# Order of work in a slot of a fused cross-attention and FP4 feed-forward kernel: maximum first on DVE, x1 a slot earlier, weights transposed last on PE

## The chip, the cores and the metric

The kernel runs on one core of a Trainium2 chip. The metric is the device time of one execution in microseconds (us). A core has a matrix engine (TensorE, PE in the profile; its weight loads are PEld), a vector engine (DVE), a scalar engine (ACT), GpSimd (POOL) and SyncE (SP), which issues all DMAs here. Each has its own instruction queue, worked off in order; they wait for one another on semaphores.

## The reference

One transformer layer with float32 inputs: x is 4 x 1024 x 256, the context 4 x 154 x 192, 16 heads of 64, a hidden width of 704.

```
n  = layernorm(x);  q = n Wq;  k, v = ctx Wk, ctx Wv          (16 heads of 64)
x1 = x + softmax(q k^T / 8) v Wo + bo
m  = layernorm(x1);  g = fp4(m) fp4(w_gate)^T;  u = fp4(m) fp4(w_up)^T
h  = silu(g) * u;    out = x1 + fp4(h) fp4(w_down)^T
```

fp4() rounds in blocks of 16 along the last axis: scale = largest magnitude / 6, values to the grid 0, 0.5, 1, 1.5, 2, 3, 4, 6, and back.

## The kernel before, in words

The 4096 rows of x are 32 tiles of 128 rows, worked in pairs; `step(pair, par)` is one tile t = 2 pair + par, written once for every engine and driven by the same `schedule`. A tile has 8 slots (k = 0 to 7), one for each pair of heads, called a unit. All float32 products are made of three: an operand is split into a high part (ACT copies PSUM to an fp32r tile: pT_hi, q_hi, xqT_hi, hqT_hi, xT_hi) and a low part (DVE subtracts that from the PSUM tile: pT_lo and so on, always L637), and PE adds hi x lo, lo x hi and hi x hi.

The tiles are software-pipelined over five tile steps. In slot k of tile t:

- PE makes the **scores** of unit k (L975, ps_s), then **attend** (L998 to L1000): the product of the softmaxed weights of the unit four slots back with B = V Wo, added up over a tile in ps_o. Then **turn_probs** (L985) transposes the weights of the unit two slots back into ps_t, a single PSUM bank, so it waits until DVE has taken the previous unit's pT_lo out of it; then come transposes of the feed-forward operands through ps_m (L865: xn in slot 1, hn in slots 4 and 5; L873: xa of two tiles in slot 6 of even tiles), a quarter of gate and up (L1015, slots 2 to 5), the down product (L1025 to L1027, 18 matmuls, slot 7), a query product of 6 matmuls (L937, slots 0, 1, 2, 4 of even and 0, 1, 3, 6 of odd tiles), and in four tiles of each batch entry the jobs that set up K, V and B of the next one.
- DVE inverts the row sums of the last unit (L746, rsum), makes pT_lo of the unit three slots back, xqT_lo (slot 2) or hqT_lo (slots 5 and 6), and only then takes the **maximum** of this slot's scores (L782, negmax). After it come xT_lo (slot 7 of even tiles), q_lo, x1 and its statistics in slot 4 (L804), the gate quarters (L752, L758, slots 3 to 6), statistics of a later tile in slot 2, and the FP4 scales and rounding (L667 to L692).
- ACT takes pT_hi first, then the other high parts, tanh of the gate quarter, and the exponential of this slot's scores (L610), which needs the maximum; y = copy of x1 (L628) in slot 3.
- POOL multiplies the weights of the last unit by the inverse sums (L472) and does the additions and scaling of the FP4 rounding (L441, L445, L447).

PE's waits inside a slot that the change touches: `attend` of a tile's first unit (slot 4) waits for x1 of the tile before, since it overwrites ps_o; the first gate product waits for xqT_lo; a query product waits for the previous query unit's q_lo; the transposes and the down product in ps_m wait for the last user of that bank (hqT_lo, xT_lo).

```
            def turn_probs(t, u):
                pe.wait_ge(norm_p, PAIRS * t + u + 1)
                if some(PAIRS * t + u):
                    pe.wait_ge(pT_lo, PAIRS * t + u)
```

Of the kernel before, what the change touches and what calls it, by code (L numbers as in the profile page):

```python
# [5 lines left out]
ALU = mybir.AluOpType  # L6
ACT = mybir.ActivationFunctionType
AX_X = mybir.AxisListType.X
# [15 lines left out]
def xattn_ffn_kernel(nc: bass.Bass, x, ctx_768, Wq, Wk, Wv, Wo, bo, w_gate, w_up, w_down, out):  # L24
# [29 lines left out]
    with ExitStack() as stack:  # L54
# [102 lines left out]
        def some(count):  # L157

            return not isinstance(count, int) or count > 0
# [351 lines left out]
        def _(act):  # L511
# [65 lines left out]
            def step(pair, par, own=True, before=True, gate=True, down=True, out_=True, ahead=True, queries=True,  # L577
                     setup=None):
                t = 2 * pair + par
                e, f, d = t - 1, t - 2, t - 3  # L580
                for k in range(SLOTS):
                    if before and k < 3:
                        weights_hi(e, k + PAIRS - 3)
                    if own and k >= 3:
                        weights_hi(t, k - 3)
                    if gate and k == 2:
                        hi_part(xqT[0][:, :, :], parts(ps_m, KT), (xqT_mm, f + 1), xqT_hi)
                    if down and k in (5, 6):
                        r = k - 5
                        hi_part(hqT[0][:, 3 * r:3 * r + 3, :], parts(ps_m, 3), (hqT_mm, 2 * d + r + 1), hqT_hi)  # L590
                    if own and ahead and par == 0 and k == 7:
                        hi_part(xT_all(0), parts(ps_m, 4), (xT_mm, pair + 2), xT_hi)
                    if own and queries and q_unit(par, k - 1) is not None:
                        q_hi_part(pair + par, q_unit(par, k - 1))
                    for job in jobs_before(setup, k):
                        take_hi(job, setup[1])
                    if gate and 3 <= k < Q + 3:
                        q = k - 3
                        quarter = slice(q * QF, (q + 1) * QF)
                        if q == 0 and not some(f):  # L600
                            act.wait_ge(raw_mm, RAW_T[CHUNKS])
                        elif q == 0:
                            act.wait_ge(hq_v, 6 * f - 2)
                        act.wait_ge(gu_mm, Q * f + q + 1)
                        act.activation(eh[:, quarter], ps_g[q % 2][:, 0:QF], ACT.Tanh, scale=0.5).then_inc(th_a, 1)
                    if own:
                        act.wait_ge(max_v, PAIRS * t + k + 1)
                        for s in range(2):
                            h = 2 * k + s
                            ins = act.activation(probs[:, h, 0:M], ps_s[k % 2][:, s * M:(s + 1) * M], ACT.Exp,  # L610
                                                 bias=negmax[:, h:h + 1], accum_out=sums[:, h:h + 1])
                        ins.then_inc(exp_a, 1)
                    if own and ahead and k == 4:
                        layer_norm1_out(t + 3, 1 - par)
                    if before and k == 5:
                        act.wait_ge(ln2_p, 2 * e + 2)
                        if some(e):
                            act.wait_ge(xqT_mm, e)
                        act.activation(xn, x1[1 - par], ACT.Identity, bias=nm2[:, :], scale=rs2[:, :])\
                           .then_inc(xln2_a, 1)  # L620
                    if turn_at(t, k, 0) is not None:
                        chunk_hi(turn_at(t, k, 0))
                    if down and k == 3:
                        at = pair - 2 + par
                        act.wait_ge(x1_v, d + 1)
                        if some(at):
                            act.wait_ge(st_y[1 - par], 16 * at)
                        act.activation(y[1 - par], x1[1 - par], ACT.Copy).then_inc(y_a, 1)  # L628
# [4 lines left out]
        def _(dve):  # L633
# [127 lines left out]
            def step(pair, par, own=True, before=True, gate=True, down=True, out_=True, ahead=True, queries=True,  # L761
                     setup=None):
                t = 2 * pair + par
                e, f, d, c = t - 1, t - 2, t - 3, t - 4
                for k in range(SLOTS):
                    if before and k == 0:
                        invert_sums(e, PAIRS - 1)
                    if own and k >= 1:
# [7 lines left out]
                    if down and k in (5, 6):  # L776
                        r = k - 5
                        lo_part(hqT[1][:, 3 * r:3 * r + 3, :], parts(ps_m, 3), hqT[0][:, 3 * r:3 * r + 3, :],
                                (hqT_hi, 2 * d + r + 1), hqT_lo)
                    if own:  # L780
                        dve.wait_ge(s_mm, PAIRS * t + k + 1)
                        dve.tensor_reduce(negmax[:, 2 * k:2 * k + 2],  # L782
                                          ps_s[k % 2][:, 0:UM].rearrange("p (h m) -> p h m", h=2),
                                          AX_X, ALU.max, negate=True).then_inc(max_v, 1)
                    if out_ and k == 0:
                        dve.wait_ge(d_mm, c + 1)
                        dve.wait_ge(y_a, c + 1)
# [7 lines left out]
                    if turn_at(t, k, 1) is not None:  # L795
                        chunk_lo(turn_at(t, k, 1))
                    if before and k == 4:
                        dve.wait_ge(o_mm, PAIRS * (e + 1))
                        dve.wait_ge(xr_p, e + 1)
                        if some(d + 1):  # L800
                            dve.wait_ge(y_a, d + 1)
                        elif not some(e):
                            dve.wait_ge(raw_mm, RAW_T[3])
                        dve.tensor_tensor(x1[1 - par], xr[1 - par][:, :], ps_o[:, 0:C], ALU.add).then_inc(x1_v, 1)  # L804
                        if some(e):
                            dve.wait_ge(xln2_a, e)
                        stats(x1[1 - par], st2, mv2, ve2, nm2, (x1_v, e + 1), ln2_v, 5 * e)
# [16 lines left out]
                    if before and k == 5:  # L824
                        dve.wait_ge(xln2_a, e + 1)
                        if some(e):
                            dve.wait_ge(xq_p, 4 * e)
                        largest(xn, xri[:, :], xq_v)
                        fp4_scales(xri[:, :], xsc[:, :], xri[:, :], xq_v, 6 * e)
                        dve.wait_ge(xq_v, 6 * e + 3)  # L830
                        dve.tensor_scalar(xri[:, :], xri[:, :], TIES_DOWN, None, ALU.mult).then_inc(xq_v, 1)
                    if gate and k == 6:
                        dve.wait_ge(h_v, Q * (f + 1))
                        largest(eh[:, 0:F], hri[:, :], hq_v)
# [18 lines left out]
        def _(pe):  # L853
# [50 lines left out]
            def make(job, b):  # L904
                kind, i, bank_ = job
                free(bank_)
                ps = BANKS[bank_]
                if kind == "V":
                    if i == 0:
                        pe.wait_ge(ld_w, 32 * b if some(b) else 32)  # L910
                    if isinstance(b, int) and i == 0:
                        pe.wait_ge(pad_p, 4)
                    project(ps, W_sb, 1, i, b, v_mm)
                if kind == "K":
                    if i == 0:
                        pe.wait_ge(ld_w, 32 * b + 16)
                    project(ps, W_sb, 0, i, b, k_mm)
                if kind in ("A", "C", "D"):
                    if isinstance(b, int) and i == 0:
                        pe.wait_ge(ld_wo, 16)  # L920
                    pe.wait_ge(v_ev, KV * b + (2 * i + 2 if kind == "D" else i + 1))
                    for n, block in enumerate(b_blocks(kind, i)):
                        ins = b_block(ps[:, n * C:(n + 1) * C], block)
                    ins.then_inc(b_mm, 1)
                held[bank_] = job_done(kind, i, b)
# [53 lines left out]
# [4 lines that stand above are left out]
                for j in range(blocks(u)):  # L983
                    at = b_at(u, j) * P
                    ins = pe.transpose(ps_t[:, j * P:(j + 1) * P], probs_rows[:, at:at + P], ident[:, :])  # L985
                ins.then_inc(t_mm, 1)
# [43 lines left out]
            def step(pair, par, own=True, before=True, gate=True, down=True, out_=True, ahead=True, queries=True,  # L1030
# [4 lines left out]
                for k in range(SLOTS):  # L1035
# [3 lines left out]
                        attend(e, k + PAIRS - 4, setup if kind == "settle" else None)  # L1039
                    if own and k >= 4:  # L1040
                        attend(t, k - 4, setup if kind in ("start", "roll") else None)
                    if before and k < 2:
                        turn_probs(e, k + PAIRS - 2)
                    if own and k >= 2:
                        turn_probs(t, k - 2)
                    if gate and k == 1:
                        pe.wait_ge(xq_p, 4 * f + 4)
                        m_free((y_v, d), (xqT_lo, f + 1))
# [24 lines left out]
                            pe.wait_ge(q_lo, PAIRS * (pair + par) + max(made))  # L1073
                    for job in jobs_at(setup, k):
                        make(job, setup[1])
                    if turn_at(t, k, 0) is not None:
                        chunk_transposes(turn_at(t, k, 0))

# [28 lines left out]
```

## Time and profile before

| what | value |
|---|---|
| median of 3 runs | 984.53 us (983.6 to 984.84) |
| the profiled execution | 986.75 us, its span 984.9 us |
| PE busy | 857.0 us, 87% of the span |
| DVE busy | 757.5 us, 77% |
| ACT, POOL busy | 534.0 us, 529.5 us |
| chain that ended last | PE 63%, DVE 21%, issue 8%, ACT 4% |
| HBM traffic | mean 23 GB/s |

The span runs from the first to the last instruction of the program, the execution's own time has 1.85 us around it. The start (two tiles) takes some 109 us, then ordinary tiles take 25 to 26 us and those that set up the next batch entry up to 36 us.

### The profile page before, as it was taken

To read this page: it belongs to the slowest core of one execution; us is meant where nothing else is said; L and a number is where in the kernel's file an instruction comes from. 1 tells how busy PE (TensorE), PEld (TensorE's weight loads), DVE (VectorE), ACT (ScalarE), POOL (GpSimd) and SP (SyncE) were. 2 spreads that over 40 slices of the span, in tenths; PEclk is the share of its full clock that TensorE was granted. 3 is DMA by queue.
4 is the path that set the end of the run, shared out by engine and by line. 5 is a ranking of instruction groups with operands and counts; after the bars stand their busy time and mean duration, and the time that the engine had idled before them with its cause. 6 is when DMAs were issued, how large, how long until landed. Compare 5 with 4: busy or idle time off the path is not lost.

```text
span 984.9 us, 21389 instructions
## 1 busy us (share of the span) xinstructions
PE 857.0 (87%) x6254; PEld 812.8 (83%) x6254; DVE 757.5 (77%) x2176; ACT 534.0 (54%) x1879; POOL 529.5 (54%) x677
## 2 busy tenths in 40 slices
PE   4786789999999999989989999989999999999874
PEld 3666789988888998888978888889888888888863
DVE  5857788877778888867878888876877888887762
ACT  4454455556565555556555555556555555655520
POOL 2545666554535656545554656554553656555651
PEclk9888999999999999999999999999999999999986
DMA  7101000001010000001000000001000000000000
GB/s 215 39 11 49 7 17 13 22 13 44 7 33 17 13 23 11 21 14 39 12 28 23 12 22 12 21 8 33 23 7 23 12 18 12 16 11 12 7 11 11
DMA packets 19869, 23.13 MB, mean 23 GB/s; under 512 B 2642, under 2 KB 18234, under 8 KB 19770
## 3 DMA queue, kind: packets, MB, share of 16 engines
q1 hardware_dynamic: 19770, 21.94, 7.2%
q8 instruction: 47, 0.77, 0.3%
q14 instruction: 52, 0.43, 0.1%
HBM read 17.74 MB, written 4.19 MB: 22 GB/s over the span
## 4 chain that ended last, share of the span: by engine, by line
PE 63%; DVE 21%; issue 8%; ACT 4%; POOL 2%; DMA 1%; DVEq 1%; SPq 0%; POOLq 0%; ACTq 0%
PE ps_g L1015 10%; PE ps_q L937 8%; PE ps_s L975 8%; PE ps_t L985 5%; PE ps_o L998 5%; PE ps_o L1000 5%; PE ps_o L999 5%; DVE negmax L782 3%; DVE pT_lo L637 3%; PE ps_m L865 3%; PE ps_g L900 3%; PE ps_m L1025 3%; PE ps_m L1027 2%; PE ps_m L1026 2%; DVE scales L667 2%
## 5 line engine op out<-in xcount | busy, mean ns | idle before, releaser
L472 POOL TENSOR_TENSOR probs<-probs,rsum 128x308 f32<-128x308 f32 x256 | 180.0, 703 | 284.2 <-DVE rsum L746 283.6
L610 ACT ACTIVATE probs<-ps_s,negmax 128x154 f32<-128x154 f32 x512 | 194.7, 386 | 229.4 <-DVE negmax L782 228.2
L998 PE MATMUL ps_o<-B_sb,pT_lo 128*128 128x256 f32 x640 | 183.6, 287 | 38.5 <-DVE x_both L804 33.9
L782 DVE TENSOR_REDUCE negmax<-ps_s 128x2 f32<-128x308 f32 x256 | 121.3, 474 | 78.4 <-PE ps_s L975 76.6
L1000 PE MATMUL ps_o<-B_sb,pT_hi 128*128 128x256 f32 x640 | 181.2, 283 | 0.0
L999 PE MATMUL ps_o<-B_sb,pT_hi 128*128 128x256 f32 x640 | 180.9, 283 | 0.0
L998 PEld LDWEIGHTS ps_o<-B_sb,pT_lo 128*128 128x128 f32 x640 | 121.7, 190 | 45.3 <-issue 42.9
L637 DVE TENSOR_TENSOR pT_lo<-ps_t,pT_hi 128x256 fp32r<-128x256 f32 (+1 forms) x256 | 122.7, 479 | 42.6 <-ACT pT_hi L514 37.4
L985 PE MATMUL ps_t<-ident,probs 128*128 128x128 f32 x640 | 115.0, 278 | 35.9 <-DVE pT_lo L637 35.3
L1015 PE MATMUL ps_g<-WGU,xqT_hi 128*128 128x352 f32 x512 | 136.6, 349 | 3.5 <-DVE B_sb L637 1.9
L514 ACT ACTIVATE pT_hi<-ps_t 128x256 fp32r<-128x256 f32 (+1 forms) x256 | 111.4, 435 | 29.1 <-PE ps_t L985 22.7
L1000 PEld LDWEIGHTS ps_o<-B_sb,pT_hi 128*128 128x128 f32 x640 | 122.1, 191 | 0.0
L999 PEld LDWEIGHTS ps_o<-B_sb,pT_hi 128*128 128x128 f32 x640 | 121.8, 190 | 0.0
L985 PEld LDWEIGHTS ps_t<-ident,probs 128*128 128x128 f32 x640 | 73.8, 141 | 47.3 <-issue 45.7
L610 ACT ACTIVATION_READ_ACCUMULATOR probs<-ps_s,negmax 128x1 f32 x512 | 100.9, 197 | 0.0
L975 PE MATMUL ps_s<-K_hi,q_lo 128*128 128x308 f32 x256 | 87.1, 340 | 3.6 <-issue 3.6
L1015 PEld LDWEIGHTS ps_g<-WGU,xqT_hi 128*128 128x128 f32 x512 | 85.3, 194 | 4.9 <-issue 2.6
L937 PE MATMUL ps_q<-xT_hi,Wq_lo 128*128 128x256 f32 x256 | 80.7, 315 | 8.7 <-DVE q_lo L637 6.1
L1015 PE MATMUL ps_g<-WGU,xqT_lo 128*128 128x352 f32 x256 | 83.5, 326 | 0.0
L441 POOL TENSOR_TENSOR hn<-hn,hc 128x704 f32<-128x704 f32 x32 | 54.4, 1700 | 50.8 <-DVE hc L692 50.8
L975 PE MATMUL ps_s<-K_hi,q_hi 128*128 128x308 f32 x256 | 78.4, 306 | 0.0
L975 PE MATMUL ps_s<-K_lo,q_hi 128*128 128x308 f32 x256 | 78.1, 305 | 0.0
(149 smaller groups left out, 2236.7 us busy)
## 6 DMA issues: line engine op xcount, KB each, us to landing
xa<-in_x_dram SPq DMA_DIRECT2D x33, 128.0 KB, 2.1
xr<-in_x_dram SPq DMA_DIRECT2D x32, 128.0 KB, 2.0
out_dram<-y_xn SPq DMA_DIRECT2D x32, 128.0 KB, 1.7
W_sb<-in_L_xattn_Wk_dram SPq DMA_DIRECT2D x4, 512.0 KB, 4.4
W_sb<-in_L_xattn_Wv_dram SPq DMA_DIRECT2D x3, 512.0 KB, 3.6
probs<-in_L_xattn_Wq_dram SPq DMA_DIRECT2D x1, 1024.0 KB, 7.0
Wo_sb<-in_L_xattn_Wo_dram SPq DMA_DIRECT2D x1, 1024.0 KB, 6.6
VT<-in_ctx_dram SPq DMA_DIRECT2D x1, 384.0 KB
```

The costliest lines, as they stand in the source:

```text
L472: pool.tensor_tensor(unit, unit, rsum[:, 2 * u:2 * u + 2].unsqueeze(2) .to_broadcast([P, 2, M]), ALU.mult).then_inc(norm_p, 1)
L514: act.activation(dst, src, ACT.Copy).then_inc(done, 1)
L610: ins = act.activation(probs[:, h, 0:M], ps_s[k % 2][:, s * M:(s + 1) * M], ACT.Exp, bias=negmax[:, h:h + 1], accum_out=sums[:, h:h + 1])
L637: dve.tensor_tensor(dst, src, hi.bitcast(F32), ALU.subtract).then_inc(done, 1)
L782: dve.tensor_reduce(negmax[:, 2 * k:2 * k + 2], ps_s[k % 2][:, 0:UM].rearrange("p (h m) -> p h m", h=2), AX_X, ALU.max, negate=True).then_ ...
L937: ins = pe.matmul(ps_q[:, 0:2 * P], Wq_sb[w][:, k, u * P:(u + 1) * P], xT[x_][:, k, :], start=(i == 0), stop=(i == len(terms) - 1))
L975: ins = pe.matmul(ps_s[u % 2][:, 0:UM], q_sb[a][:, u, par * P:(par + 1) * P], K_sb[b][:, u, :], start=(i == 0), stop=(i == len(terms) - 1))
L985: ins = pe.transpose(ps_t[:, j * P:(j + 1) * P], probs_rows[:, at:at + P], ident[:, :])
L998: pe.matmul(ps_o[:, 0:C], lo[:, j, :], w[:, 0:C], start=first, stop=False)
L999: pe.matmul(ps_o[:, 0:C], hi[:, j, :], w[:, C:2 * C], start=False, stop=False)
L1000: ins = pe.matmul(ps_o[:, 0:C], hi[:, j, :], w[:, 0:C], start=False, stop=last)
L1015: ins = pe.matmul(ps_g[q % 2][:, 0:2 * QF], x_[:, k, :], WGU[:, k, a, :, q * QF:(q + 1) * QF], start=(i == 0), stop=(i == len(terms) - 1))
```

## The change

It moves three things and adds or removes nothing. On DVE the maximum of a slot's scores comes first in the slot, ahead of the reciprocal and of all low parts. x1 is written as the last DVE work of slot 3 and no longer in slot 4 (its statistics stay there); ACT's copy of x1 into y moves with it from slot 3 to slot 2. On PE `turn_probs` comes behind all products and jobs of the slot. Line numbers move with it: L782 becomes L768, L804 becomes L832, L985 L986 and so on.

```diff
--- before.py
+++ after.py
@@ -620,7 +620,7 @@
                            .then_inc(xln2_a, 1)
                     if turn_at(t, k, 0) is not None:
                         chunk_hi(turn_at(t, k, 0))
-                    if down and k == 3:
+                    if down and k == 2:
                         at = pair - 2 + par
                         act.wait_ge(x1_v, d + 1)
                         if some(at):
@@ -763,6 +763,11 @@
                 t = 2 * pair + par
                 e, f, d, c = t - 1, t - 2, t - 3, t - 4
                 for k in range(SLOTS):
+                    if own:
+                        dve.wait_ge(s_mm, PAIRS * t + k + 1)
+                        dve.tensor_reduce(negmax[:, 2 * k:2 * k + 2],
+                                          ps_s[k % 2][:, 0:UM].rearrange("p (h m) -> p h m", h=2),
+                                          AX_X, ALU.max, negate=True).then_inc(max_v, 1)
                     if before and k == 0:
                         invert_sums(e, PAIRS - 1)
                     if own and k >= 1:
@@ -777,11 +782,6 @@
                         r = k - 5
                         lo_part(hqT[1][:, 3 * r:3 * r + 3, :], parts(ps_m, 3), hqT[0][:, 3 * r:3 * r + 3, :],
                                 (hqT_hi, 2 * d + r + 1), hqT_lo)
-                    if own:
-                        dve.wait_ge(s_mm, PAIRS * t + k + 1)
-                        dve.tensor_reduce(negmax[:, 2 * k:2 * k + 2],
-                                          ps_s[k % 2][:, 0:UM].rearrange("p (h m) -> p h m", h=2),
-                                          AX_X, ALU.max, negate=True).then_inc(max_v, 1)
                     if out_ and k == 0:
                         dve.wait_ge(d_mm, c + 1)
                         dve.wait_ge(y_a, c + 1)
@@ -795,13 +795,6 @@
                     if turn_at(t, k, 1) is not None:
                         chunk_lo(turn_at(t, k, 1))
                     if before and k == 4:
-                        dve.wait_ge(o_mm, PAIRS * (e + 1))
-                        dve.wait_ge(xr_p, e + 1)
-                        if some(d + 1):
-                            dve.wait_ge(y_a, d + 1)
-                        elif not some(e):
-                            dve.wait_ge(raw_mm, RAW_T[3])
-                        dve.tensor_tensor(x1[1 - par], xr[1 - par][:, :], ps_o[:, 0:C], ALU.add).then_inc(x1_v, 1)
                         if some(e):
                             dve.wait_ge(xln2_a, e)
                         stats(x1[1 - par], st2, mv2, ve2, nm2, (x1_v, e + 1), ln2_v, 5 * e)
@@ -829,6 +822,14 @@
                         fp4_scales(xri[:, :], xsc[:, :], xri[:, :], xq_v, 6 * e)
                         dve.wait_ge(xq_v, 6 * e + 3)
                         dve.tensor_scalar(xri[:, :], xri[:, :], TIES_DOWN, None, ALU.mult).then_inc(xq_v, 1)
+                    if before and k == 3:
+                        dve.wait_ge(o_mm, PAIRS * (e + 1))
+                        dve.wait_ge(xr_p, e + 1)
+                        if some(d + 1):
+                            dve.wait_ge(y_a, d + 1)
+                        elif not some(e):
+                            dve.wait_ge(raw_mm, RAW_T[3])
+                        dve.tensor_tensor(x1[1 - par], xr[1 - par][:, :], ps_o[:, 0:C], ALU.add).then_inc(x1_v, 1)
                     if gate and k == 6:
                         dve.wait_ge(h_v, Q * (f + 1))
                         largest(eh[:, 0:F], hri[:, :], hq_v)
@@ -1039,10 +1040,6 @@
                         attend(e, k + PAIRS - 4, setup if kind == "settle" else None)
                     if own and k >= 4:
                         attend(t, k - 4, setup if kind in ("start", "roll") else None)
-                    if before and k < 2:
-                        turn_probs(e, k + PAIRS - 2)
-                    if own and k >= 2:
-                        turn_probs(t, k - 2)
                     if gate and k == 1:
                         pe.wait_ge(xq_p, 4 * f + 4)
                         m_free((y_v, d), (xqT_lo, f + 1))
@@ -1073,6 +1070,10 @@
                             pe.wait_ge(q_lo, PAIRS * (pair + par) + max(made))
                     for job in jobs_at(setup, k):
                         make(job, setup[1])
+                    if before and k < 2:
+                        turn_probs(e, k + PAIRS - 2)
+                    if own and k >= 2:
+                        turn_probs(t, k - 2)
                     if turn_at(t, k, 0) is not None:
                         chunk_transposes(turn_at(t, k, 0))
```

The first place is DVE in slot 2 of an even tile of the steady loop, before and now (with what each row waits for; negmax is the maximum, rsum the reciprocal):

```order
L746 RECIPROCAL rsum<-sums 128x2 [waits exp_a]
L637 TENSOR_TENSOR pT_lo<-ps_t,pT_hi 128x384 [waits pT_hi]
L637 TENSOR_TENSOR xqT_lo<-ps_m,xqT_hi 128x256 [waits xqT_hi]
L781 REGISTER_ALU
L782 TENSOR_REDUCE negmax<-ps_s 128x2 [waits s_mm]
```

```order
L768 TENSOR_REDUCE negmax<-ps_s 128x2 [waits s_mm]
L746 RECIPROCAL rsum<-sums 128x2 [waits exp_a]
L637 TENSOR_TENSOR pT_lo<-ps_t,pT_hi 128x384 [waits pT_hi]
L637 TENSOR_TENSOR xqT_lo<-ps_m,xqT_hi 128x256 [waits xqT_hi]
L636 REGISTER_ALU
L637 TENSOR_TENSOR q_lo<-ps_q,q_hi 128x256 [waits q_hi]
```

The maximum, which waits for the scores of this slot (s_mm), now stands ahead of the two low parts. In slots 5 and 6 it stands in the same way ahead of hqT_lo.

The second place is DVE around the boundary of slots 3 and 4, before and now (x_both is x1):

```order
L758 SCALAR_TENSOR_TENSOR eh<-ps_g,gu 128x176 [waits silu_v]
L746 RECIPROCAL rsum<-sums 128x2 [waits exp_a]
L637 TENSOR_TENSOR pT_lo<-ps_t,pT_hi 128x384 [waits pT_hi]
L781 REGISTER_ALU
L782 TENSOR_REDUCE negmax<-ps_s 128x2 [waits s_mm]
L804 TENSOR_TENSOR x_both<-xr,ps_o 128x256 [waits y_a,xr_p,o_mm]
```

```order
L758 SCALAR_TENSOR_TENSOR eh<-ps_g,gu 128x176 [waits silu_v]
L832 TENSOR_TENSOR x_both<-xr,ps_o 128x256 [waits y_a,xr_p,o_mm]
L767 REGISTER_ALU
L768 TENSOR_REDUCE negmax<-ps_s 128x2 [waits s_mm]
L746 RECIPROCAL rsum<-sums 128x2 [waits exp_a]
L637 TENSOR_TENSOR pT_lo<-ps_t,pT_hi 128x384 [waits pT_hi]
```

x1 has moved ahead of the maximum of slot 4.

The third place is PE in slot 2 of that tile, from the last attend matmuls on, before and now:

```order
L1000 MATMUL ps_o<-B_sb,pT_hi 128x256
L985 MATMUL ps_t<-ident,probs 128x128 [waits pT_lo,norm_p]
L985 MATMUL ps_t<-ident,probs 128x128
L1008 REGISTER_ALU [waits xqT_lo]
L1015 MATMUL ps_g<-WGU,xqT_hi 128x352 [waits h_v]
```

```order
L1001 MATMUL ps_o<-B_sb,pT_hi 128x256
L1009 REGISTER_ALU [waits xqT_lo]
L1016 MATMUL ps_g<-WGU,xqT_hi 128x352 [waits h_v]
...
L938 MATMUL ps_q<-xT_hi,Wq_hi 128x256
L986 MATMUL ps_t<-ident,probs 128x128 [waits pT_lo,norm_p]
L986 MATMUL ps_t<-ident,probs 128x128
L973 REGISTER_ALU [waits q_lo]
```

The transposes of the weights have moved from ahead of the gate product to the slot's end, behind the query product.

## Rows read from the trace of the kernel before

**Rows 1.** Windows view, core 0: one even and the following odd tile (bounds, length, busy us and instructions of each engine, granted clock, DMA share, GB/s).
```profile
559.50:585.50 26.00, 23.84 (x183) 22.83 (x183) 22.45 (x67) 15.03 (x55) 16.03 (x22) 1.00 0.07 22
585.50:610.60 25.10, 23.08 (x181) 22.51 (x180) 20.54 (x62) 14.54 (x54) 14.86 (x20) 1.00 0.04 12
```

**Rows 2.** List of waits, whole span (who waited for whom: us in total, times, longest us).
```profile
PE ps_t L985 <- DVE pT_lo L637: 35.3, 40, 3.2
PE ps_o L998 <- DVE x_both L804: 33.9, 28, 2.4
```

**Rows 3.** Timeline, slot 1 of tile 18 (start us, us, engine, line, operation, out<-in, count).
```profile
561.52 0.30 PE L975 MATMUL ps_s<-K_hi,q_lo 128*128 128x308 f32 x1
...
563.47 0.36 PE L937 MATMUL ps_q<-xT_hi,Wq_lo 128*128 128x256 f32 x1
```

**Rows 4.** Timeline, slot 2 of tile 18, PE and DVE.
```profile
564.06 0.56 DVE L637 TENSOR_TENSOR pT_lo<-ps_t,pT_hi 128x384 fp32r<-128x384 f32 x1 [0.35 <-ACT pT_hi L514]
...
564.26 0.31 PE L975 MATMUL ps_s<-K_hi,q_lo 128*128 128x308 f32 x1
...
564.53 0.41 DVE L637 TENSOR_TENSOR xqT_lo<-ps_m,xqT_hi 128x256 fp32r<-128x256 f32 x1
...
564.89 0.48 DVE L782 TENSOR_REDUCE negmax<-ps_s 128x2 f32<-128x308 f32 x1
...
565.54 0.56 PE L1015 MATMUL ps_g<-WGU,xqT_hi 128*128 128x352 f32 x2
```

**Rows 5.** Timeline, slot 4 of tile 18, and the same product in tile 19; brackets: idle before.
```profile
570.09 0.30 PE L975 MATMUL ps_s<-K_hi,q_lo 128*128 128x308 f32 x1
...
571.66 0.35 PE L998 MATMUL ps_o<-B_sb,pT_lo 128*128 128x256 f32 x1 [0.99 <-DVE x_both L804]
...
598.06 0.36 PE L998 MATMUL ps_o<-B_sb,pT_lo 128*128 128x256 f32 x1 [1.32 <-DVE x_both L804]
```

**Rows 6.** Timeline, end of slot 4 and slot 5 of tile 18, PE and DVE.
```profile
573.73 0.56 DVE L637 TENSOR_TENSOR hqT_lo<-ps_m,hqT_hi 128x384 fp32r<-128x384 f32 x1
...
574.68 0.30 PE L975 MATMUL ps_s<-K_hi,q_lo 128*128 128x308 f32 x1
...
575.30 0.48 DVE L782 TENSOR_REDUCE negmax<-ps_s 128x2 f32<-128x308 f32 x1 [1.01 <-PE ps_s L975]
...
576.17 0.49 PE L985 MATMUL ps_t<-ident,probs 128*128 128x128 f32 x3
...
576.50 0.49 PE L865 MATMUL ps_m<-ident,hn 128*128 128x128 f32 x3
```

**Rows 7.** Timeline, slots 6 and 7 of tile 18, PE and DVE.
```profile
578.85 0.55 DVE L637 TENSOR_TENSOR hqT_lo<-ps_m,hqT_hi 128x384 fp32r<-128x384 f32 x1
...
581.76 0.16 DVE L746 RECIPROCAL rsum<-sums 128x2 f32<-128x2 f32 x1
...
582.39 0.52 PE L985 MATMUL ps_t<-ident,probs 128*128 128x128 f32 x3 [0.80 <-DVE pT_lo L637]
582.54 0.68 DVE L637 TENSOR_TENSOR xT_lo<-ps_m,xT_hi 128x512 fp32r<-128x512 f32 x1
...
583.28 0.39 PE L1025 MATMUL ps_m<-WD,hqT_lo 128*128 128x256 f32 x1 [0.37 <-DVE xT_lo L637]
```

**Rows 8.** Timeline, slot 7 of tile 19, PE and DVE.
```profile
608.07 0.52 PE L985 MATMUL ps_t<-ident,probs 128*128 128x128 f32 x3 [0.70 <-DVE pT_lo L637]
608.23 0.41 DVE L637 TENSOR_TENSOR q_lo<-ps_q,q_hi 128x256 fp32r<-128x256 f32 x1
...
610.56 0.15 DVE L746 RECIPROCAL rsum<-sums 128x2 f32<-128x2 f32 x1
```

**Rows 9.** Timeline, slot 2 of tile 18, POOL beside DVE.
```profile
565.79 1.71 POOL L445 TENSOR_TENSOR hn<-hn,hc 128x704 f32<-128x704 f32 x1
...
566.36 1.15 DVE L664 TENSOR_TENSOR small<-small 128x1 f32<-128x1 f32 x1
```

## The prediction

> **What bounds the kernel now.** I read the windows view first. In an even tile of the steady loop TensorE (PE) is busy 23.84 of 26.00 us, in the odd tile after it 23.08 of 25.10; DVE has 22.45 and 20.54 us of work there, ACT and POOL 14.5 to 16.0, and the granted clock is 1.00 [rows 1]. So PE sets the pace and about 4 us of a pair are its idle time. The list of waits says for what: for the attention weights' low part (pT_lo) in front of the transposes, 35.3 us in the whole span, and for x1 in front of the first product into ps_o, 33.9 us [rows 2]. Both are waits for DVE. What matters next is when, inside a slot, DVE delivers each thing, and for that I read the timeline of one pair, tiles 18 and 19. All offsets below are from the start of a slot's scores (L975) on PE.
>
> **What goes.** x1 is written behind the maximum of slot 4. PE's first L998 there starts 1.57 after the scores; where it need not wait it starts 0.43 after them, so 1.14 is wait (gap 0.99 in the row, plus 0.15 of pipelined tail) [rows 5]. The odd tile shows a gap of 1.32, hence 1.47. With x1 as the last DVE work of slot 3 it starts at 0.62 (maximum) + 0.40 + 0.08 (reciprocal) + 0.38 (pT_lo) + 0.34 (q_lo) + 0.37 + 0.30 (gate quarter) = 2.49 and ends at 2.90; slot 3 is 2.80 long and PE asks at 0.43 of slot 4, 3.23. So this wait goes, with 0.2 to spare: 2.6 a pair. In slot 7 the transposes wait for pT_lo 0.80 + 0.15 in the even tile [rows 7] and 0.70 + 0.15 in the odd one [rows 8]; there pT_lo is late because DVE's work of slot 6 runs past the scores. With the transposes behind the down product (18 matmuls, over 2 us) both go: 1.8. The wait of the down product for xT_lo in the even slot 7 (583.28 against 582.39 + 0.25: 0.64) and 0.36 of small waits in the two slots 6 are counted below against what takes their place. Old waits of a pair: 2.6 + 1.8 + 0.64 + 0.36 = 5.4 us.
>
> **What comes.** Before, DVE did the low parts ahead of the maximum, so it worked on them in the tail of the slot before, while PE was still busy there: xqT_lo runs 0.27 to 0.69 after the scores of slot 2 and the gate product, which needs it, starts at 1.28 [rows 4]; the first hqT_lo starts at 573.73, before the scores of slot 5 at 574.68 [rows 6]. Now the maximum stands first and waits for this slot's scores. That wait ends 0.62 after the scores' start (575.30 against 574.68) [rows 6]. The maximum takes 0.48 and the next starts some 0.08 before an end (564.06 + 0.56 against 564.53) [rows 4]: reciprocal at 1.02, pT_lo at 1.10, the next low part at 1.48 or, behind three blocks, 1.57. From a DVE end to PE's start I take 0.14 to 0.15. Everything that PE needs inside the same slot, behind its scores and one attend product, is now late:
> - Slot 1, q_lo: 1.48 + 0.41 + 0.15 = 2.04. PE asks at 1.95, less the 0.32 of the transposes that stood ahead: 1.63 [rows 3]. Wait 0.40, in both tiles.
> - Slot 2, xqT_lo: 1.57 + 0.41 + 0.14 = 2.12. PE asks at 1.28 - 0.14 = 1.14. Wait 0.98, in both [rows 4].
> - Slot 5, first hqT_lo: 1.48 + 0.56 + 0.14 = 2.16 or so; PE asks where the transposes of the weights stood, 576.17, which is 1.49 [rows 6]. Wait 0.66, in both.
> - Slot 6 of the even tile, second hqT_lo: 1.57 + 0.56 + 0.14 = 2.27 against 1.14 for the two-tile transposes of xa. Wait 1.13.
> - Slot 7 of the even tile, xT_lo. From hqT_lo's start to the next reciprocal DVE took 581.76 - 578.85 = 2.91, of which 0.39 is the maximum, now ahead [rows 7]. So it is free at 1.57 + 2.52 = 4.09 of a slot that is 2.83 long: 1.26 into slot 7. Then 0.40 + 0.08 + 0.38 + 0.68 (xT_lo) + 0.14 = 2.94, against the down product's 1.50. Wait 1.44.
> - Odd tile: slot 6 is 2.06 long, so DVE is 2.0 late in slot 7, which costs PE nothing there (hqT_lo is done, the transposes come last, at 3.65). But 2.03 + 0.86 + 2.33 (q_lo to the next reciprocal, 610.56 - 608.23 [rows 8]) is 1.3 past a slot of 3.92, and the transposes of the next slot 0, now at its end, wait some 0.4; slot 5 begins about 0.25 late because slot 4 without the x1 wait is only 2.6 long. Together 0.7.
>
> New waits of a pair: 0.80 + 1.96 + 1.32 + 1.13 + 1.44 + 0.7 = 7.4. Against them stands that three transposes ahead of other transposes cost 0.33 (576.17 to 576.50) [rows 6] and at a slot's end some 0.25; an estimate of 0.06 a slot gives 0.5. Net: 7.4 - 5.4 - 0.5 = **+1.5 us a pair**.
>
> **Edits priced at nothing.** POOL gets a unit's reciprocal later, but the transposes of it come a slot later still; its hn steps end 0.6 before PE asks in slot 4. ACT's copy of x1 into y moves to slot 2, where ACT idles. The rotation of pT_hi on ACT: the transposes now end 0.2 after the next scores start, pT_hi ends by 0.7, DVE wants it at 1.10; if that cover failed, pT_lo and all behind it would slip with it. No queue of DMAs moves.
>
> **The sum.** 15 pairs behind the start at +1.5 are +22. The start pair has some 13 of the 35.3 us for pT_lo, because it idles long in slots that are DVE's; transposes put last free part of it, between 0 and 6, I take -3. The last pair has no xa transposes and no queries: -1. So +18 on the profiled execution's 986.75 us gives 1004.8; the median of the runs stands 2.2 lower, so I forecast 1002.5 for it, slower by 1.8%. Bounds: a wait of PE costs at least nothing and each of the six new ones is good to about 0.15 (the spread of the offsets between the two tiles), together 0.8 a pair or 12 us: 991 to 1014.
>
> **A rule against the row.** In slot 2 DVE's last small operation (L664) took 1.15 us, not the 0.15 it takes elsewhere, and ended when POOL's hn operation did, 565.79 + 1.71 [rows 9]. So POOL can hold DVE for a whole instruction. The Trainium skill ("SBUF — State Buffer", "SBUF: two separate sides") says so: the shared port pair is an exclusive lock, taken also by a DVE operation with two SBUF inputs, and the loser fully blocks. The trace agrees with that in these two rows. By the sum this changes nothing, since slot 2 has that much slack left; by the rule a later DVE queue meets other POOL instructions, which is the second rival.
>
> **The rivals.**
> 1. *Backlog dissolves* (faster). PE's new waits in slots 1, 2 and 5 give DVE time; if DVE reaches slot 7 early in both tiles, the 1.44 of xT_lo falls to 0.3, slot 6's 1.13 to 0.6 and the odd tile's 0.7 goes. That is 2.4 less: -0.9 a pair, -14 and -4, or 966. For it: DVE has 3.5 to 4.5 us free in a tile [rows 1]. Against: this slack lies ahead of slots 5 and 6, whose offsets count from the scores, and does not help behind them. It decides if xT_lo ends before 2.2 of slot 7.
> 2. *POOL holds DVE* (slower still). One meeting as in rows 9 on the path in each pair costs 1.0: +15 more, 1017.
> 3. *Even trade.* The new waits are 5.9 a pair: no change, 984.5.
> 4. *Only the removed waits count*, DVE's order costs PE nothing: 15 pairs lose 4.4 to 5.4, 66 to 81 us: 903 to 918. It would need PE's products in slots 2 and 5 not to wait for low parts, against their semaphores.
>
> **Chances.** Forecast 0.62, with 991 to 1014 as its own range; rival 2 0.14; rival 3 0.06; rival 1 0.14; rival 4 0.04. Less than 0.2% (2 us) can't be told from no change. So slower 0.76, same 0.06, faster 0.18. The range runs from 974, which takes in part of rival 1, to 1018.
>
> **What would show it.** Right: L998 of slot 4 without a gap; the L1016 row of ps_g (gate product) waiting about 1.0 for xqT_lo in every tile, L866 for the first hqT_lo 0.5 to 0.9, the xa transposes over 1 for the second, the down product of even tiles over 1 for xT_lo; pairs of 52 to 53 us against 51.1; DVE's maximum starting 0.6 behind the scores with idle time before it. Wrong: gate products that start at 1.15, or a pair under 51.

## The result, and the profile after

| | before | changed |
|---|---|---|
| median of 4 runs | 984.1 us (983.6 to 984.84) | 1011.37 us (1008.73 to 1014.25) |
| the profiled execution, its span | 986.75 us, 984.9 us | 1009.81 us, 1007.9 us |

The changed kernel is slower by 2.8%: ratio 1.0277, 95% interval 1.0244 to 1.031. The forecast was 1002.5 us, 1.8% slower, with 974 to 1018 as its range. One execution of a kernel below (after_largest) was a disturbed one, of 1674.6 us with scores matmuls of 0.51 us where they usually take 0.30; it is left out of that kernel's time.

The page of the changed kernel, its head and the chain that ended last:

```profile
span 1007.9 us, 21398 instructions
...
PE 860.6 (85%) x6254; PEld 809.2 (80%) x6254; DVE 731.2 (73%) x2176; ACT 520.9 (52%) x1879; POOL 541.8 (54%) x677
...
issue 38%; POOL 35%; PE 12%; DVE 11%; POOLq 1%; ACT 1%; DMA 1%; SPq 0%; DVEq 0%; ACTq 0%
```

The span is 23 us longer. PE has the same matmuls: it is busy 3.6 us more and idle 19.4 us more (147.3 against 127.9). The chain is a trap here: it was 63% PE before and is now 35% POOL, whose 542 us fill 54% of the span. POOL now waits for 212 of the 256 reciprocals (133 before), so the chain, followed back from wait to wait, runs along it; low_first below shows that it doesn't bind.

The list of waits of the changed kernel (whole span, as [rows 2]):

```profile
ACT pT_hi L514 <- PE ps_t L986: 319.7, 243, 4.2
DVE negmax L768 <- PE ps_s L976: 205.0, 182, 3.7
...
PE ps_g L1016 <- DVE xqT_lo L637: 20.1, 25, 1.0
...
PE ps_t L986 <- DVE pT_lo L637: 17.2, 13, 4.3
...
PE ps_m L1026 <- DVE xT_lo L637: 13.0, 13, 1.3
...
PE ps_m L866 <- DVE hqT_lo L637: 12.1, 31, 1.2
PE ps_m L874 <- DVE hqT_lo L637: 11.1, 13, 0.9
PE ps_q L938 <- DVE q_lo L637: 10.8, 14, 2.9
```

Of the 33.9 us for x1 1.5 are left, and of the 35.3 us for pT_lo in [rows 2] 17.2, nearly all in the start (12.0) and the last tiles (2.8). In their place stand five waits inside the slots. DVE now waits 205 us for scores (76.6 before) and ACT 320 us for the transposes (22.7 before). The windows of tiles 18 and 19, as [rows 1]:

```profile
572.60:600.30 27.70, 24.22 (x186) 23.07 (x184) 22.15 (x65) 14.84 (x55) 17.90 (x23) 1.00 0.07 21
600.30:624.70 24.40, 23.21 (x181) 22.51 (x179) 18.85 (x62) 14.17 (x54) 14.02 (x19) 1.00 0.04 12
```

The even tile became 1.6 us longer, the odd one 0.65 us shorter: 52.05 against 51.11 us, +0.94 for the pair. Slot 2 of tile 18, which answers to [rows 4], from the timelines of PE, ACT and DVE:

```profile
578.16 0.39 PE L976 MATMUL ps_s<-K_hi,q_lo 128*128 128x308 f32 x1
...
578.44 0.49 ACT L514 ACTIVATE pT_hi<-ps_t 128x384 fp32r<-128x384 f32 x1 [1.23 <-PE ps_t L986]
...
578.67 0.28 PE L999 MATMUL ps_o<-B_sb,pT_lo 128*128 128x256 f32 x1
...
578.87 0.48 DVE L768 TENSOR_REDUCE negmax<-ps_s 128x2 f32<-128x308 f32 x1 [1.29 <-PE ps_s L976]
...
579.34 0.54 DVE L637 TENSOR_TENSOR pT_lo<-ps_t,pT_hi 128x384 fp32r<-128x384 f32 x1
579.79 0.41 DVE L637 TENSOR_TENSOR xqT_lo<-ps_m,xqT_hi 128x256 fp32r<-128x256 f32 x1
...
580.33 0.58 PE L1016 MATMUL ps_g<-WGU,xqT_hi 128*128 128x352 f32 x2 [0.80 <-DVE xqT_lo L637]
```

DVE stands still for 1.29 us in front of the maximum, then does maximum, pT_lo and xqT_lo in a row, and PE starts the gate product 2.17 after the scores. The other three places, slots 5, 6 and 7 of the same tile, which answer to [rows 6, 7]:

```profile
590.52 0.55 PE L866 MATMUL ps_m<-ident,hn 128*128 128x128 f32 x3 [0.36 <-DVE hqT_lo L637]
...
594.35 0.66 PE L874 MATMUL ps_m<-ident,xa 128*128 128x128 f32 x4 [0.85 <-DVE hqT_lo L637]
...
597.79 0.39 PE L1026 MATMUL ps_m<-WD,hqT_lo 128*128 128x256 f32 x1 [1.08 <-DVE xT_lo L637]
```

### The profile page after: what moved, and what is told of

It is laid out like the page before. It is cut to its first block, busy times and chain, and to the rows that moved or that the text cites. A ratio compares the mean times of both kernels' runs of the same rounds, so it can differ in the third digit from the quotient of the medians.

```text
span 1007.9 us, 21398 instructions
## 1 busy us (share of the span) xinstructions
PE 860.6 (85%) x6254; PEld 809.2 (80%) x6254; DVE 731.2 (73%) x2176; ACT 520.9 (52%) x1879; POOL 541.8 (54%) x677
## 4 chain that ended last, share of the span: by engine, by line
issue 38%; POOL 35%; PE 12%; DVE 11%; POOLq 1%; ACT 1%; DMA 1%; SPq 0%; DVEq 0%; ACTq 0%
POOL probs L472 8%; POOL hn L445 4%; POOL hn L441 4%; POOL hn L447 3%; POOL y_xn L445 3%; PE ps_g L1016 3%; POOL small L453 3%; POOL xr L493 2%; POOL y_xn L441 2%; POOL y_xn L447 2%; DVE negmax L768 2%; PE ps_s L976 2%; PE ps_q L938 2%; POOL y_xn L503 2%; DVE pT_lo L637 1%
## 5 line engine op out<-in xcount | busy, mean ns | idle before, releaser
L768 DVE TENSOR_REDUCE negmax<-ps_s 128x2 f32<-128x308 f32 x256 | 121.6, 475 | 205.1 <-PE ps_s L976 205.0
L999 PE MATMUL ps_o<-B_sb,pT_lo 128*128 128x256 f32 x640 | 181.1, 283 | 1.5 <-DVE x_both L832 1.5
L1016 PE MATMUL ps_g<-WGU,xqT_hi 128*128 128x352 f32 x512 | 133.1, 341 | 28.8 <-DVE xqT_lo L637 20.1
L986 PE MATMUL ps_t<-ident,probs 128*128 128x128 f32 x640 | 113.0, 275 | 17.3 <-DVE pT_lo L637 17.2
L637 DVE TENSOR_TENSOR pT_lo<-ps_t,pT_hi 128x256 fp32r<-128x256 f32 (+1 forms) x256 | 120.3, 470 | 0.9 <-ACT pT_hi L514 0.9
L1016 PEld LDWEIGHTS ps_g<-WGU,xqT_hi 128*128 128x128 f32 x512 | 84.4, 191 | 35.3 <-issue 28.3
L610 ACT ACTIVATION_READ_ACCUMULATOR probs<-ps_s,negmax 128x1 f32 x512 | 105.6, 206 | 0.0
L976 PE MATMUL ps_s<-K_hi,q_lo 128*128 128x308 f32 x256 | 99.7, 389 | 6.4 <-issue 6.4
L986 PEld LDWEIGHTS ps_t<-ident,probs 128*128 128x128 f32 x640 | 79.4, 141 | 24.5 <-issue 20.2
L938 PE MATMUL ps_q<-xT_hi,Wq_lo 128*128 128x256 f32 x256 | 77.1, 301 | 16.2 <-DVE q_lo L637 10.8
L938 PE MATMUL ps_q<-xT_lo,Wq_hi 128*128 128x256 f32 x256 | 73.0, 285 | 0.0
```

What stands on the lines that cost most here:

```text
L637: dve.tensor_tensor(dst, src, hi.bitcast(F32), ALU.subtract).then_inc(done, 1)
L768: dve.tensor_reduce(negmax[:, 2 * k:2 * k + 2], ps_s[k % 2][:, 0:UM].rearrange("p (h m) -> p h m", h=2), AX_X, ALU.max, negate=True).then_ ...
L938: ins = pe.matmul(ps_q[:, 0:2 * P], Wq_sb[w][:, k, u * P:(u + 1) * P], xT[x_][:, k, :], start=(i == 0), stop=(i == len(terms) - 1))
L976: ins = pe.matmul(ps_s[u % 2][:, 0:UM], q_sb[a][:, u, par * P:(par + 1) * P], K_sb[b][:, u, :], start=(i == 0), stop=(i == len(terms) - 1))
L999: pe.matmul(ps_o[:, 0:C], lo[:, j, :], w[:, 0:C], start=first, stop=False)
L1016: ins = pe.matmul(ps_g[q % 2][:, 0:2 * QF], x_[:, k, :], WGU[:, k, a, :, q * QF:(q + 1) * QF], start=(i == 0), stop=(i == len(terms) - 1))
```

## The experiments

Theory A, of the prediction: PE waits for a low part as long as that part's place in DVE's slot, counted from the scores, lies behind the point where PE asks; the maximum put first shifts all places. Against it stand that the transposes at the slot's end do the harm (they make pT_hi, and with it everything queued behind, late), and that POOL or the engines' total work bind. In the expectations of the first four runs these are T1 (theory A), T2 (the transposes) and T3 (POOL).

**One part and two parts of the change.** Four kernels on one chip; before, there, 984.26 us.

x_alone is x1 in slot 3 and ACT's copy in slot 2, nothing else:

```diff
-                    if before and k == 4:
-                        dve.wait_ge(o_mm, PAIRS * (e + 1))
...
+                    if before and k == 3:
+                        dve.wait_ge(o_mm, PAIRS * (e + 1))
...
-                    if down and k == 3:
+                    if down and k == 2:
```

> Only x1 a slot earlier (with ACT's copy), DVE and PE in the old order. If PE's waits for x1 are simply PE time (T1 and all theories): 28 waits of 1.1 to 1.5 us go, 984 - 35 = 946 to 952. If DVE's 0.4 us of x1 in slot 3 only moves the wait to pT_lo or q_lo of slot 4: 975 to 984.

Measured: 946.26 us, ratio 0.9602 (0.957 to 0.9634). This part alone takes 4% off. The timeline of its tile 18, scores of slot 4 and what follows on PE, and x1 on DVE:

```profile
549.16 0.41 DVE L832 TENSOR_TENSOR x_both<-xr,ps_o 128x256 f32<-128x256 f32 x1
...
549.98 0.30 PE L976 MATMUL ps_s<-K_hi,q_lo 128*128 128x308 f32 x1
...
550.40 0.28 PE L999 MATMUL ps_o<-B_sb,pT_lo 128*128 128x256 f32 x1
```

x1 ends 0.4 before the scores of slot 4, and the product follows them at 0.42, with no gap where [rows 5] had 0.99.

x_max is the change with the transposes at their old place (the edit against the change):

```diff
+                    if before and k < 2:
+                        turn_probs(e, k + PAIRS - 2)
+                    if own and k >= 2:
+                        turn_probs(t, k - 2)
                     if gate and k == 1:
...
                         make(job, setup[1])
-                    if before and k < 2:
-                        turn_probs(e, k + PAIRS - 2)
-                    if own and k >= 2:
-                        turn_probs(t, k - 2)
```

> The change without its third part: maximum first, x1 in slot 3, transposes of the weights at their old place ahead of the products. T1 (maximum first holds every low part of the slot behind the scores): the transposes now ask for pT_lo at 1.14 or 1.49 of the slot and get it at 1.66 to 1.77, a new wait of 0.2 to 0.6 in every slot and 1.6 in odd slots 7: 10 us of waits a pair, 1045 to 1060. T2 (what costs is that transposes at the slot's end make pT_hi and so all behind it late): with them early again it should be faster than the change, under 985. T3 (POOL, which gets its reciprocal later, is the bound): as the change, 1005 to 1015.

Measured: 1042.58 us, ratio 1.0593 (1.0568 to 1.0619). With the transposes early again the kernel is slower than the change, not faster, so T2 and T3 as the only cause fall. T1 holds in kind, 2 us below its range: the gaps are 0.39 to 0.48 in even slots, and the 1.6 that I wrote for odd slots 7 did not come (0.70, as before). The new wait, slot 2 of its tile 18, on PE:

```profile
595.33 0.30 PE L976 MATMUL ps_s<-K_hi,q_lo 128*128 128x308 f32 x1
...
597.10 0.41 PE L986 MATMUL ps_t<-ident,probs 128*128 128x128 f32 x2 [0.48 <-DVE pT_lo L637]
597.42 0.58 PE L1016 MATMUL ps_g<-WGU,xqT_hi 128*128 128x352 f32 x2
```

The transposes start 1.77 after the scores, the figure of the expectation.

x_last is the change with the maximum at its old place, behind the low parts; against the kernel before only `turn_probs` and x1 move (of which `turn_probs` is shown):

```diff
-                    if before and k < 2:
-                        turn_probs(e, k + PAIRS - 2)
-                    if own and k >= 2:
-                        turn_probs(t, k - 2)
...
                     for job in jobs_at(setup, k):
                         make(job, setup[1])
+                    if before and k < 2:
+                        turn_probs(e, k + PAIRS - 2)
+                    if own and k >= 2:
+                        turn_probs(t, k - 2)
```

> The change without its first part: transposes last, x1 in slot 3, maximum in its old place behind the low parts. T1: the low parts wait only for pT_hi (0.7 of the slot) and not for scores and maximum, so waits in slots 2, 5 and 6 shrink from 0.98, 0.5 and 1.0 to 0.5, 0.2 and 0.7: 4.5 us of waits a pair, 960 to 972. T2: no better than the change, 1000 to 1012. T3: POOL gets its reciprocals as before, 985 or less.

Measured: 1006.38 us, ratio 1.0241 (1.0213 to 1.0269). Here my theory missed by 34 us, and T2's number was hit. ACT and DVE queues of its slot 2, and PE:

```profile
571.45 0.39 PE L976 MATMUL ps_s<-K_hi,q_lo 128*128 128x308 f32 x1
...
571.73 0.49 ACT L514 ACTIVATE pT_hi<-ps_t 128x384 fp32r<-128x384 f32 x1 [0.84 <-PE ps_t L986]
572.12 0.38 ACT L514 ACTIVATE xqT_hi<-ps_m 128x256 fp32r<-128x256 f32 x1
...
572.25 0.56 DVE L637 TENSOR_TENSOR pT_lo<-ps_t,pT_hi 128x384 fp32r<-128x384 f32 x1 [1.17 <-ACT pT_hi L514]
572.73 0.41 DVE L637 TENSOR_TENSOR xqT_lo<-ps_m,xqT_hi 128x256 fp32r<-128x256 f32 x1
...
573.27 0.42 PE L1016 MATMUL ps_g<-WGU,xqT_hi 128*128 128x352 f32 x1 [0.45 <-DVE xqT_lo L637]
```

With the transposes last, pT_hi can start only 0.28 after the next scores; DVE idles 1.17 in front of pT_lo, and xqT_lo behind it is late although its own operand lay in ps_m a slot before. So there are two blocks at the head of DVE's slot, the scores (for the maximum) and pT_hi (for pT_lo), and they overlap: with x1 moved, maximum first adds 96 us (946 to 1043), transposes last add 60 (946 to 1006), both together 65 (946 to 1011).

max_last_x4 is the change with x1 left in slot 4 (both moves of x_alone taken back, DVE's and ACT's):

> The change with x1 left in slot 4. x1 then stands behind this slot's maximum, reciprocal, pT_lo and q_lo and ends 1.98 to 2.3 after the scores, PE asks at 0.43: a wait of 1.7 in even and 2.0 in odd tiles, 31 tiles: 1011 + 55 = 1055 to 1075. If a wait in slot 4 only takes over those of slots 5 to 7 (all theories in which DVE's sum of work is the bound): 1015 to 1030.

Measured: 1087.11 us, ratio 1.104 (1.0998 to 1.1082). The wait in slot 4 of its tile 18 has a gap of 1.51, in tile 19 of 1.85; with the 0.15 of tail that is the 1.7 and 2.0 expected. The total is 12 us above my range. The list of waits has 48.3 us for x1 in 28 waits, some 52 with their tails, and the profiled executions are 79.9 us apart (1089.72 and 1009.81). What is missing fits TensorE's clock, granted at 0.954 on average here and at 0.980 in the change. The windows view from the scores of slot 4 of tile 19 on (columns as in [rows 1]):

```profile
659.16:662.70 3.54, 1.69 (x15) 1.47 (x14) 2.65 (x11) 2.22 (x8) 1.38 (x4) 1.00 0.01 4
662.70:666.10 3.40, 3.40 (x16) 3.33 (x15) 0.45 (x3) 0.74 (x3) 0.66 (x2) 0.50 0.14 39
666.10:669.07 2.97, 2.70 (x21) 2.48 (x21) 2.80 (x10) 1.58 (x7) 0.70 (x1) 1.00 0.00 0
```

PE was busy for 1.69 of 3.54 us, with the wait in it, and then worked 3.4 us at a clock of 0.50 (1.2 instead of 2.4 GHz). Slots 4 and 5 of this tile are together 3.5 us longer than in the change, 1.5 more than the wait. The kernel has 18 such stretches more than the change, an estimate of 27 us, which with the 52 gives the 79. So a wait of PE can cost more than its own length.

**The places tested one by one.** Six more kernels (before 984.29 and 983.98 us in their two sets, on two other chips).

low_first is the change with xqT_lo, hqT_lo and xT_lo moved between the maximum and the reciprocal, ahead of pT_lo:

```diff
                                           AX_X, ALU.max, negate=True).then_inc(max_v, 1)
+                    if gate and k == 2:
+                        lo_part(xqT[1][:, :, :], parts(ps_m, KT), xqT[0][:, :, :], (xqT_hi, f + 1), xqT_lo)
+                    if down and k in (5, 6):
+                        r = k - 5
...
+                    if own and ahead and par == 0 and k == 7:
+                        lo_part(xT_all(1), parts(ps_m, 4), xT_all(0), (xT_hi, pair + 2), xT_lo)
                     if before and k == 0:
                         invert_sums(e, PAIRS - 1)
```

> The change, with the feed-forward low parts (and xT_lo in slot 7) between the maximum and the reciprocal, so ahead of pT_lo. Theory A (each new wait of PE is the place of that low part in DVE's slot, counted from the scores): xqT_lo is there 0.5 earlier, hqT_lo 0.3 to 0.4, xT_lo 0.45; in odd slots 6 pT_lo comes after the transposes ask, +0.45: -2.1 a pair, 975 to 985. Theory B (the loss is DVE's and ACT's sum of work or their latency loop, not the place): 1006 to 1014, as the change.

Measured: 989.36 us, ratio to before 1.0039 (1.0015 to 1.0062): 22 us less than the change with the same work on every engine, for 26 to 36 expected (4 above my range). Theory B falls. The slot 2 of its tile 18:

```profile
568.95 0.48 DVE L768 TENSOR_REDUCE negmax<-ps_s 128x2 f32<-128x308 f32 x1 [1.31 <-PE ps_s L976]
569.34 0.41 DVE L637 TENSOR_TENSOR xqT_lo<-ps_m,xqT_hi 128x256 fp32r<-128x256 f32 x1
...
569.89 0.59 PE L1016 MATMUL ps_g<-WGU,xqT_hi 128*128 128x352 f32 x2 [0.27 <-DVE xqT_lo L637]
```

The wait fell from 0.80 to 0.27, by the 0.5 that pT_lo takes.

after_largest is the change with DVE's reduction over the hidden row (L667, 0.89 us a piece) moved from slot 6 to slot 7, in front of its scales:

```diff
-                    if gate and k == 6:
-                        dve.wait_ge(h_v, Q * (f + 1))
-                        largest(eh[:, 0:F], hri[:, :], hq_v)
...
                     if gate and k == 7:
+                        dve.wait_ge(h_v, Q * (f + 1))
+                        largest(eh[:, 0:F], hri[:, :], hq_v)
                         if some(f):
```

> The change, with the reduction over the hidden row (L667, 0.81 us) moved from slot 6 to slot 7, behind the low parts and in front of its scales. Theory A: DVE is no longer late in slot 7, xT_lo comes 0.5 earlier in even tiles (wait 1.08 to 0.6), the rest of the change's waits stay: -0.5 a pair, 1000 to 1006. Theory B: nothing, since DVE has the same work: 1009 to 1014.

Measured: 997.3 us (the median of four, 995.16 to 1001.33), ratio 1.0131 (1.0074 to 1.0187), 14 us less than the change, 3 below my range. No trace of it can show the wait in slot 7, so the reading rests on the time.

low_largest joins the two edits:

> low_first (989 us) with the reduction over the hidden row in slot 7. By the places: the wait of 1.01 in the even slot 7 falls by 0.5 to 0.8, the 0.37 of the odd slot 6 stays: 977 to 984. If the reduction's place gives nothing once the low parts stand first: 987 to 991.

Measured: 982.01 us, ratio 0.9976 (0.9959 to 0.9993). In its timeline the wait for xT_lo in the even slot 7 is 0.35 where low_first has 1.01. That is all three parts of the change at the speed of the kernel before, with only the places of low parts and of one reduction altered.

x_last_ff tests the miss of x_last: there, ACT and DVE now do the feed-forward parts and xT ahead of pT_hi and pT_lo. On ACT:

```diff
+                    if gate and k == 2:
+                        hi_part(xqT[0][:, :, :], parts(ps_m, KT), (xqT_mm, f + 1), xqT_hi)
...
                     if before and k < 3:
                         weights_hi(e, k + PAIRS - 3)
```

> As x_last (transposes last, x1 in slot 3, maximum behind the low parts: 1006 us), with the feed-forward parts and xT first in their slots on ACT and DVE, ahead of pT_hi and pT_lo. If transposes last cost because every high and low part of the slot stands in its in-order queue behind pT_hi, which can start only 0.3 after the scores: the waits of slots 2 (0.45 and 0.51), 5 (0.10), 6 (1.02) and part of 7 (1.47) go, 3.3 a pair, 955 to 965. If they cost through PE itself (scores behind transposes 0.08 later, 16 a pair) or through the maximum and exponential coming later: 995 or more.

Measured: 971.44 us, ratio 0.987 (0.9836 to 0.9903): 35 us less than x_last, 6 above my range and far from the 995 of the other causes. The waits of slots 2 and 5 are gone from its timeline, that of slot 6 is 0.24. The parts were late because of what stood ahead of them in their queues. ACT's order and DVE's were changed together, so which of the two queues mattered more is not shown. Left are 0.65 for q_lo in slot 1, 0.81 for pT_lo in the odd slot 6 and 1.01 for xT_lo. The pair is 1.0 us longer than in x_alone (49.8 against 48.8), the tiles behind a new batch entry 2.5 (36.7 against 34.2), which is most of the 25 us between them.

**A version that beats both.** x_largest is x_alone with the reduction moved to slot 7.

> x1 in slot 3 alone (946 us), with the reduction over the hidden row moved to slot 7. Theory A: the only waits left there are 0.78 and 0.37 of slot 7 (even), 0.36 and 0.67 of slots 6 and 7 (odd); pT_lo and xT_lo come 0.81 earlier, so 1.9 to 2.3 of a pair go: 912 to 922. Theory B: 940 to 948.

Measured: 928.57 us, ratio 0.9426 (0.9381 to 0.9472), 5.7% less than before, some 8% less than the change. Slot 7 of its tile 18, DVE and PE:

```profile
547.66 0.42 DVE L637 TENSOR_TENSOR pT_lo<-ps_t,pT_hi 128x256 fp32r<-128x256 f32 x1
...
548.24 0.52 PE L985 MATMUL ps_t<-ident,probs 128*128 128x128 f32 x3
548.39 0.68 DVE L637 TENSOR_TENSOR xT_lo<-ps_m,xT_hi 128x512 fp32r<-128x512 f32 x1
548.99 0.88 DVE L667 TENSOR_REDUCE scales<-eh 128x44 f32<-128x704 f32 x1
549.13 0.39 PE L1025 MATMUL ps_m<-WD,hqT_lo 128*128 128x256 f32 x1 [0.37 <-DVE xT_lo L637]
```

pT_lo is early enough, and the gap of 0.80 in front of the transposes [rows 7] is gone. I had expected 912 to 922, 7 us too little. The 0.37 for xT_lo stayed, since the transposes, now earlier, bring the asking point forward by as much as xT_lo; in the odd slot 6 a gap of 0.34 for pT_lo stayed too, and slot 0 of even tiles grew from 2.06 to 2.35 us.

x_lg_odd7 adds to it the transposes behind the down product in slot 7 of odd tiles alone:

> As x_largest, and in odd tiles alone the transposes of slot 7 behind the down product. Theory A: their wait is gone already; they now end 0.3 after the next scores start, so pT_hi and pT_lo of slot 0 come late, but nothing on PE asks for them before its end: within 3 us of x_largest. If transposes last cost by themselves (pT_hi late, the scores behind transposes 0.08 later): 2 to 8 us slower than x_largest.

Measured: 927.37 us against 928.57: no difference that can be told. Transposes last cost nothing where nobody asks soon for what is queued behind pT_hi.

## Why the prediction was right, and where it was off

**What goes: right.** L998 of slot 4 has no gap left, and x_alone shows the part by itself: 38 us for the 2.6 a pair that I wrote (39 in 15 pairs). The waits of slot 7 for pT_lo went in both tiles, as written.

**What comes: right in kind and mostly in size.** Every wait on my list is in the trace, at its place and for its tile. With the 0.15 of tail added to each gap: slot 1 0.53 in even tiles (I wrote 0.40) and no gap in odd ones, whose slot 1 is 0.28 longer all the same; slot 2 0.95 in both (0.98); slot 5 0.51 and 0.53 (0.66); slot 6 1.00 (1.13); slot 7 1.23 (1.44). The 0.7 for DVE's backlog in odd tiles did not come: slot 5 is 3.69 and 3.71 us long in the two tiles and slot 0 of the even one 2.14. Together 5.7 where I had 7.4.

**The credit of 0.5 was wrong.** I let the transposes at a slot's end cost PE less. They cost the scores behind them more: the second scores matmul starts 0.22 after the first (578.16, 578.38), where it was 0.14 (561.52, 561.66), and attend comes at 0.51 instead of 0.43. But this is moved and not new. Before, the product behind the transposes paid it (the second query matmul of slot 0 starts 0.20 after the first, 560.73 and 560.93, in place of 0.12), and the first matmul behind transposes starts 0.03 after the last of them instead of 0.11. Such changes went from 16 to 22 a pair and cost 0.14 more together. Counted by the starts of matmuls, with the short waits that show no gap and the slower start behind a wait, the old waits of the pair are 5.75 and the new ones 6.49. That is +0.74 of waits and +0.14 of changes, and nearly all of the +0.94; I had +2.0, less the credit.

**The rest of the sum was off the other way.** On the profiled executions the forecast was +18 us and +23.1 came. By starts of tiles: five ordinary pairs +0.8 to +0.95 each as above, the three that make V and K of the next entry +1.3 to +1.5, tiles 2 and 3 -0.6; the three pairs that set up K, V and B behind a new batch entry +2.7 each, with more of the same kind of wait: the gate product of slot 2 waits 1.72 (0.64 before) for the low part of B (B_sb) in its PSUM bank, which now stands behind the maximum, pT_lo and xqT_lo, the first query product of the next tile waits 1.40 for another (0.65), and slots 6 and 7 grew by 1.8; two pairs in front of a loop's end +2.3 and +2.4, of which 1.3 and 1.4 is a longer standstill at the loop's end, marked as issue; the start and the first two tiles +1.3, for which I took -3 (PE's waits for pT_lo there are 12.0 us before and after); the last two +0.8, for which I took -1, because the transposes wait there for pT_lo in slots 0 and 6. I priced start, end and set-up tiles without rows of their own; that step, not the mechanism, is the 5 us. There is luck in its being only 5: 15 pairs at +0.94 instead of +1.5 made my sum 8 us too high, the tiles without rows 13 too low.

The medians differ by 27 us, the profiled executions by 23. The profiled execution before was granted a clock of 0.973 and the changed one 0.980, four stretches of 3.4 us at half clock less; at the 1.5 us a stretch of max_last_x4 that is up to 6 us, an estimate, that the 23 leaves out. The changed kernel's executions spread over 5.5 us, and the two longer ones (1012.93 and 1014.25 us) were granted 0.971, the others 0.975 and 0.980.

**The rivals.** POOL as the bound is refuted by low_first: there the reciprocal, and with it POOL's product, comes 0.33 us later in slot 2 (the reciprocal 0.72 after the maximum's start, not 0.39) and the kernel is 22 us faster. That the backlog dissolves did not happen: xT_lo ended 2.76 after the scores, not before 2.2. That POOL holds DVE on the path (rival 2) did not show. L673 took 0.68 us at 597.66 in the change and 0.28 in x_alone, beside POOL's rounding of xn, but no wait of PE in the pair hangs on it. Rivals 3 and 4 (984.5, and 903 to 918) fall with the time.

**What the prediction missed** is that the transposes' place matters by itself. It named pT_hi as a cover of 0.4 us ("if that cover failed, pT_lo and all behind it would slip"); the cover held only because the maximum stood ahead. x_last, where it doesn't, lost 60 us against x_alone in another way. As tested, theory A had only the maximum as a block; its ranges held in three of the ten runs (x_alone, low_largest, x_lg_odd7) and were missed in the other seven, by 34 us in x_last and by 2 to 12 us in the rest, which all went the way that it gives.

## What to carry to other kernels

In engines that work their queues in order, sort each slot's work by when its operand is ready and when its result is asked for; an operation on the newest data (here the maximum over this slot's scores) put first delays all that was ready before it, by the whole of its wait. Test the parts of a combined change apart: here one part was worth -38 us and the two that came with it cost +65. Look as well for long work that nobody needs soon (the reduction over the hidden row): moved behind what PE waits for, it gave 18 us more.

## What was not expected of the hardware

- Between the first and the second of the scores matmuls lie 0.22 us where they follow transposes and 0.14 where they follow the query product. Nothing is lost by it: the first of them starts 0.03 us behind the last transpose, not 0.11. PE meets it wherever transposes end, 16 times in the pair before and 22 times now.
- In max_last_x4 TensorE's clock fell to 0.50 for 3.4 us in many steady tiles behind the longer wait in slot 4. Before and in the change this happened between 125 and 950 us only once, at the first loop's end.
- The standstill of PE at the end of the inner loop differs between orders of the same instructions: 1.6 to 2.3 us in the four traces with transposes early, 2.0 to 3.3 in the six with transposes last, 1.8 and 2.2 in x_lg_odd7. No run explains it. Before and changed, the first scores behind it:

```profile
436.83 0.52 PE L975 MATMUL ps_s<-K_hi,q_lo 128*128 128x308 f32 x1 [1.98 <-issue]
```

```profile
445.91 0.40 PE L976 MATMUL ps_s<-K_hi,q_lo 128*128 128x308 f32 x1 [3.29 <-issue]
```
